# Features in 32-row groups, contexts of the second attention in four column tiles, late expert loads by ScalarE, and new orders in a two-layer language-model tower

## The reference, cut to what matters

```python
h = take(table, x)                                    # 16 sequences of 128 tokens, 256 channels
h = h + attn0(layernorm(h))                           # causal linear attention, 16 heads of 16: elu+1 features
h = h + ffn0(layernorm(h))                            # one 256x256 product, scaled weights
h = h + attn1(layernorm(h))                           # below
h = h + moe(layernorm(h))                             # shared expert and top-1 of 8 experts

def softmax_kernel(x, proj, is_query):                # attn1's features: 16 heads x 64
    xp = einsum('bhnd,md->bhnm', x * 16 ** -0.25, proj)
    diag = sum(square(x), -1, keepdims=True) * 0.5 * 0.25
    stab = max(xp, -1) if is_query else max(xp, (-1, -2))
    return (exp(xp - diag - stab) + 1e-4) / 8
k_sum = sum(kp, axis=2)
denom = einsum('bhnm,bhm->bhn', qp, k_sum)
ctx = einsum('bhnm,bhnd->bhmd', kp, v)
out = einsum('bhnm,bhmd->bhnd', qp, ctx) / denom
x = layer_norm(video + out @ Wo.T + bo, g2, be2)      # then relu MLP of width 1024 and layer_norm again

score = sigmoid(max(logits)); xs = x * score          # moe
h = silu(xs @ gate_e) * (xs @ up_e); moe_out = h @ down_e     # e = argmax of the logits
return moe_out + (silu(x @ shared_gate) * (x @ shared_up)) @ shared_down
```

## Time and profile before

| | |
|---|---|
| runs of the kernel before | 719.12, 720.42, 721.68 us, median 720.42 |
| the profiled execution's own time | 719.09 us |
| its span, first to last instruction | 717.3 us |
| mean granted TensorE clock | 0.979 of full |
| TensorE, VectorE, ScalarE, GpSimd busy | 666.2, 488.2, 282.2, 272.2 us |
| tower; experts | to about 566 us; 151 us |

### The profile page before, as it was taken

The page is one execution under the profiler, slowest core; times in us unless marked ns, Lnnn a source line. Parts: engine busy times, 40 slices in busy tenths (PEclk is TensorE's granted clock), DMA queues, the critical chain, the costliest instruction groups (busy, mean ns, idle before and its releaser), DMA issues.

```text
span 717.3 us, 15031 instructions
## 1 busy us (share of the span) xinstructions
PE 666.2 (93%) x5626; PEld 545.7 (76%) x5627; DVE 488.2 (68%) x1116; ACT 282.2 (39%) x664; POOL 272.2 (38%) x422
## 2 busy tenths in 40 slices
PE   3879899999999999999999999999938699999996
PEld 3667688888898898989888898899937365565654
DVE  1888999999889888888878977867525122323231
ACT  2345456546454462636355263454201032322221
POOL 6244344525426153342504325314201344454542
PEclk9999999999999999999999999999979799999998
DMA  7940000000011010000000000000063411012110
GB/s 266 417 181 9 2 10 8 9 9 9 8 17 16 17 9 16 1 16 9 9 16 1 17 8 9 17 16 8 9 191 117 119 38 48 27 41 66 54 54 11
DMA packets 17296, 34.18 MB, mean 48 GB/s; under 512 B 7617, under 2 KB 12240, under 8 KB 15952
## 3 DMA queue, kind: packets, MB, share of 16 engines
q1 hardware_dynamic: 12640, 24.89, 10.0%
q0 software_dynamic: 4592, 8.41, 4.7%
HBM read 28.74 MB, written 7.29 MB: 50 GB/s over the span
## 4 chain that ended last, share of the span: by engine, by line
PE 79%; DVE 7%; DMA 4%; issue 4%; POOL 3%; ACT 2%; SPq 0%; POOLq 0%; DVEq 0%; ACTq 0%
PE ps L1070 74%; PE ps L1075 2%; DMA x_rows<-send_x 2%; PE ps L1240 2%; DMA sorted_ids<-tokens,slot_u 1%; DVE S_sb L770 1%; DVE stats L711 1%; ACT qkA L687 1%; POOL rstd L412 1%; ACT yTB L677 1%; POOL H L380 1%; POOL preC L471 0%; DMA yA<-x_rows,ids 0%; POOL sorted_ids L483 0%; DVE yA L716 0%
## 5 line engine op out<-in xcount | busy, mean ns | idle before, releaser
L411 POOL TENSOR_TENSOR var_eps<-mv,ln_eps 128x1 f32<-128x1 f32 x112 | 27.7, 248 | 270.3 <-DVE mv L712 269.6
L1070 PE MATMUL ps<-yTC,we 128*128 128x128 f32 x1024 | 125.3, 277 | 0.5 <-DVE yTA L798 0.5
L1070 PEld LDWEIGHTS ps<-yTC,we 128*128 128x128 f32 x1024 | 120.5, 194 | 1.4 <-issue 1.0
L1070 PE MATMUL ps<-we,yTA 128*128 128x256 f32 (+1 forms) x288 | 96.9, 469 | 3.1 <-issue 1.5
L1070 PEld LDWEIGHTS ps<-we,yTA 128*128 128x128 f32 x288 | 54.3, 199 | 27.7 <-issue 22.1
L1070 PE MATMUL ps<-we,yTB 128*128 128x256 f32 (+1 forms) x216 | 71.8, 466 | 0.0
L412 POOL TENSOR_TENSOR rstd<-var_eps,pow_half 128x1 f32<-128x1 f32 x112 | 64.4, 575 | 8.8
L1070 PE MATMUL ps<-we,ffT 128*128 128x256 f32 x256 | 62.0, 385 | 0.0
L1070 PEld LDWEIGHTS ps<-we,yTB 128*128 128x128 f32 x216 | 40.3, 190 | 23.8 <-issue 21.0
L1070 PEld LDWEIGHTS ps<-we,ffT 128*128 128x128 f32 x256 | 46.2, 190 | 8.2 <-issue 3.2
L770 DVE TENSOR_TENSOR S_sb<-ps,causal_sb 128x512 f32<-128x512 f32 x64 | 40.5, 678 | 8.1 <-PE ps L1070 8.1
(11 more groups left out here) (183 smaller groups left out, 1329.1 us busy)
## 6 DMA issues: line engine op xcount, KB each, us to landing
...
x_rows<-send_x SPq DMA_DIRECT2D x16, 128.0 KB, 1.7
home_rows<-send_home SPq DMA_DIRECT2D x16, 128.0 KB, 1.7
...
we<-w_experts SPq DMA_DIRECT2D x3, 512.0 KB, 3.9
we<-w_qk SPq DMA_DIRECT2D x2, 512.0 KB, 3.7
...
```

The source lines that it names most:

```text
L411: link(pool.tensor_tensor(var_eps[:, k:k + 1], mv[:, k, 1:2], ln_eps[:], ALU.add))
L1070: return pe.matmul(o, a, b, start=start, stop=stop)
```

## The change

- `features` works in four groups of 32 rows with proj_sb as a block diagonal of two heads (32 rows, 128 columns). b_k and b_q become one step b_kq with 16 matmuls; the features fill half of each of banks 0 to 3 for K and the other half for Q (xka, xkb). b_rk copies them in two instructions, b_qs reduces and subtracts in two halves each.
- The contexts have [v, 1] of a head (32 columns) as stationary value and its 64 K features as moving one, in four column tiles: one step b_ctx with 16 matmuls. The result is transposed the wrong way round, so ScalarE copies it (b_cT), and two transposes (b_cTT) bring it to ctxp, from where b_cx and b_cx2 copy as before.
- a_den does both halves in one matmul of 256 columns: 8 matmuls.
- free_b, free_ff, free_ga, free_up and free_dn move from SyncE's list to ScalarE's, the loads with them.
- Constants other than four are set by VectorE. TensorE runs 48 f16 matmuls into a free bank before its first step.
- All lists get new orders and lags (TensorE's largest lag is 11, so 27 passes), PSUM a new map, and the `after` waits are laid anew to suit.

```diff
+    WARMING = 48
...
-        proj_sb = sb("proj_sb", [P, 4 * M])
+        proj_sb = sb("proj_sb", [P, 2 * M])
...
-        voB = sb("voB", [P, PAIRS, 2, 32])
+        voB = sb("voB", [P, HEADS, 2, DH])
...
+        ctxT_sb = sb("ctxT_sb", [P, D])
...
-        dgT, T0, qk0, v0, nd0, o0 = (ps[:, 7, :], ps[:, 0, :], ps[:, 3, :], ps[:, 5, :], ps[:, 4, :], ps[:, 3, :])
-        T2, ff0, T3, qk1, v1, dg = (ps[:, 3, :], ps[:, 7, :], ps[:, 6, :], ps[:, 6, :], ps[:, 7, :], ps[:, 6, :])
-        ctxp, nd1, o1, T5, fa, fb = (ps[:, 0, :], ps[:, 0, :], ps[:, 2, :], ps[:, 7, :], ps[:, 7, :], ps[:, 2, :])
-        f2, T6, lo, ga, up, cn = (ps[:, 3, :], ps[:, 7, :], ps[:, 5, :], ps[:, 4, :], ps[:, 2, :], ps[:, 5, :])
-        dn, km, kb = (ps[:, 1, :], ps[:, 5, :], ps[:, 6, :])
-        sc = [ps[:, 6, :], ps[:, 5, :], ps[:, 1, :], ps[:, 2, :]]
-        xk = ps[:, 6:8, :]
-        xq = ps[:, 0:2, :]
+        dgT, T0, qk0, v0, nd0, o0 = (ps[:, 7, :], ps[:, 6, :], ps[:, 6, :], ps[:, 7, :], ps[:, 3, :], ps[:, 4, :])
+        T2, ff0, T3, qk1, v1, dg = (ps[:, 6, :], ps[:, 2, :], ps[:, 4, :], ps[:, 4, :], ps[:, 5, :], ps[:, 6, :])
+        ctxp, ctxT, nd1, o1, T5, fa = (ps[:, 7, :], ps[:, 5, :], ps[:, 4, :], ps[:, 4, :], ps[:, 1, :], ps[:, 7, :])
+        fb, f2, T6, lo, ga, up = (ps[:, 5, :], ps[:, 6, :], ps[:, 5, :], ps[:, 2, :], ps[:, 0, :], ps[:, 1, :])
+        cn, dn, km, kb = (ps[:, 3, :], ps[:, 3, :], ps[:, 7, :], ps[:, 7, :])
+        sc = [ps[:, 5, :], ps[:, 0, :], ps[:, 1, :], ps[:, 2, :]]
         qT = ps[:, 1:3, :]
+        xka = ps[:, 0:2, :]
+        xkb = ps[:, 2:4, :]
...
-                (5, home_out), (0, free_ff), (4, free_ga), (8, ids3), (7, ids1), (2, x_out), (3, ids0), (3, free_up),
-                (2, free_b), (5, free_dn), (7, ids2),
+                (0, x_out), (8, ids2), (2, ids0), (5, ids1), (3, home_out), (8, ids3),
...
-                (7, r4), (4, pA), (6, hC), (10, scat), (4, r1), (4, r2), (1, gat), (0, r0), (8, r5), (4, pA2),
-                (8, r6), (4, r3), (5, pB), (7, pC),
+                (6, pA2), (5, pA), (8, r4), (7, pB), (11, scat), (7, hC), (6, r3), (9, r5), (5, r1), (8, pC), (9, r6),
+                (1, r0), (5, r2), (1, gat),
...
+            def b_cT(t):
+
+                act.wait_ge(S["ctxT_psum"], t + 1)
+                act.activation(ctxT_sb[:], ctxT[:, 0:D], ACT.Copy).then_inc(S["ctxT_ready"], 1)
...
-                act.wait_ge(S["xk_psum"], t + 1)
-                after(act, "ctx_psum", t)
-                act.activation(flat(kf[:]), flat(xk), ACT.Copy).then_inc(S["xk_read"], 1)
+                act.wait_ge(S["xkq_psum"], t + 1)
+                for half, banks in enumerate((xka, xkb)):
+                    act.activation(by_bank(kf, half), banks[:, :, D:2 * D], ACT.Copy).then_inc(S["xk_read"], 1)
...
+            def load_experts(first, last, done):
+                for e in range(first, last):
+                    act.dma_start(we[:, e * EXPERT:(e + 1) * EXPERT], w_experts[e]).then_inc(S[done], 16)
+
+            def free_b(t):
+
+                if t == T - 1:
+                    act.wait_ge(S["ffn0_psum"], T)
+                    act.wait_ge(S["out1_psum"], T)
+                    load_experts(RESIDENT, freed_by_b, "experts_loaded")
+
+            def free_ff(t):
+
+                if t == T - 1:
+                    act.wait_ge(S["ff2_psum"], 2 * T)
+                    load_experts(freed_by_b, freed_by_ff, "experts_loaded")
...
-                (6, b_cx2), (1, a_x), (9, c_tt), (5, b_dgc), (4, a_yT2), (10, c_th), (7, c_ra), (9, c_send),
-                (7, c_rb), (0, a_yT), (5, b_ek), (4, b_yT), (5, b_keps), (1, a_exp), (2, a_rd), (8, c_yT2), (5, b_eq),
-                (6, c_yT), (4, b_x), (4, b_sq), (5, b_rqT), (1, a_par), (4, b_rk),
+                (10, c_th), (2, a_rd), (5, b_cT), (4, b_yT), (8, c_tt), (1, a_par), (0, a_yT), (5, b_rqT), (4, b_x),
+                (5, b_cx2), (4, b_sq), (0, a_x), (4, b_dgc), (4, b_rk), (6, c_ra), (3, a_yT2), (13, free_dn),
+                (8, c_send), (6, c_rb), (5, free_b), (4, b_ek), (4, b_keps), (12, free_up), (7, free_ff), (0, a_exp),
+                (7, c_yT2), (11, free_ga), (4, b_eq), (5, c_yT),
...
-                x = xq.rearrange("p b (h m) -> p (b h) m", m=M)
-                dve.wait_ge(S["xq_psum"], t + 1)
-                link(dve.tensor_reduce(qmax[:, 0, :], x, AX.X, ALU.max))
+                dve.wait_ge(S["xk_read"], t * 2 + 2)
+                halves = [banks[:, :, 0:D].rearrange("p b (h m) -> p b h m", m=M) for banks in (xka, xkb)]
+
+                def heads_of(v, half):
+                    return v[:, 8 * half:8 * half + 8].rearrange("p (b h) -> p b h", b=2)
+                dve.tensor_reduce(heads_of(qmax[:, 0, :], 0), halves[0], AX.X, ALU.max).then_inc(S["dve_step"], 1)
+                counted()
+                link(dve.tensor_reduce(heads_of(qmax[:, 0, :], 1), halves[1], AX.X, ALU.max))
                 dve.wait_ge(S["diag_read"], t + 1)
                 link(dve.tensor_tensor(by_group(qmax[:, 1, :]), by_group(qmax[:, 0, :]), diag_of(0), ALU.add))
-                dve.tensor_tensor(qf[:], x, by_head(qmax[:, 1, :], M), ALU.subtract).then_inc(S["qexp_in"], 1)
+                for half in range(2):
+                    dve.tensor_tensor(by_bank4(qf, half), halves[half],
+                                      heads_of(qmax[:, 1, :], half).unsqueeze(3).broadcast_to([P, 2, 4, M]), ALU.subtract
+                                      ).then_inc(S["qexp_in"], 1)
...
-                (4, a_o), (7, b_o), (6, b_vo), (6, b_ks), (5, b_norm), (10, table1), (6, b_qs), (7, b_x1),
-                (0, a_stats), (2, a_max), (4, a_res), (11, c_hid), (2, a_elu), (2, a_vz), (10, table2), (8, c_o),
-                (3, a_rec), (4, a_norm2), (0, a_norm), (3, a_mean), (6, b_cx), (9, c_log), (9, c_choose), (5, b_km),
-                (8, c_res), (2, a_m1), (10, table3), (2, a_m3), (2, a_m0), (6, b_rec), (5, kmx), (2, a_m2),
-                (6, b_mean), (8, c_norm), (5, b_dgr), (9, c_slot), (4, a_ff), (10, c_gc), (9, table0), (11, c_down),
+                (10, c_norm), (7, b_ks), (7, b_vo), (8, b_x1), (11, c_slot), (12, table2), (13, c_hid), (6, a_ff),
+                (9, c_o), (5, a_o), (6, b_norm), (3, a_elu), (11, table0), (12, table3), (10, c_log), (9, c_res),
+                (12, c_gc), (1, a_stats), (3, a_vz), (5, a_res), (4, a_rec), (5, a_norm2), (4, a_mean), (3, a_m1),
+                (11, table1), (7, b_cx), (3, a_m2), (3, a_m3), (13, c_down), (3, a_m0), (1, a_norm), (10, c_choose),
+                (7, b_rec), (2, a_max), (7, b_mean), (6, b_dgr), (6, b_km), (6, b_qs), (6, kmx), (7, b_o),
...
-                for half in range(2):
-                    for a in range(2):
-                        for b in range(4):
-                            ins = matmul(nd0[32 * b:32 * b + 32, D + half * P:D + half * P + P], flat(den_oneA[:, a]),
-                                         S_sb[:, b, 2 * half + a, :], a == 0, a == 1)
+                for a in range(2):
+                    for b in range(4):
+                        ins = matmul(nd0[32 * b:32 * b + 32, D:2 * D].rearrange("p (h n) -> p h n", h=2), flat(den_oneA[:, a]),
+                                     S_sb[:, b].rearrange("p (h a) n -> p a h n", a=2)[:, a], a == 0, a == 1)
...
-            def features(banks, first_chunk):
+            def features(at, first_chunk):
 
                 for c in range(KD):
-                    for g in range(2):
-                        rows_of = slice(64 * g, 64 * g + 64)
-                        ins = matmul(banks[:, g, c * 4 * M:(c + 1) * 4 * M],
+                    for g in range(4):
+                        rows_of = slice(32 * g, 32 * g + 32)
+                        ins = matmul((xka, xkb)[g // 2][:, g % 2, at + c * P:at + c * P + P],
                                      qkB[rows_of, first_chunk + c, :], proj_sb[rows_of, :], True, True)
...
-            def b_k(t):
+            def b_kq(t):
 
                 if t == 0:
                     pe.wait_ge(S["weights_scaled"], 3)
                 pe.wait_ge(S["qk1_ready"], t * 4 + 4)
-                features(xk, KD).then_inc(S["xk_psum"], 1)
-
-            def b_q(t):
-                pe.wait_ge(S["qk1_ready"], t * 4 + 4)
-                if t + 5 < T:
-                    after(pe, "src0T_ready", t + 6)
-                after(pe, "tile_done", t - 5)
-                features(xq, 0).then_inc(S["xq_psum"], 1)
+                if t + 3 < T:
+                    after(pe, "scores_masked", (t + 3) * 4 + 3)
+                after(pe, "tile_done", t - 6)
+                features(D, KD)
+                features(0, 0).then_inc(S["xkq_psum"], 1)
...
-            def contexts(t, quarter):
-
-                for pair in range(2 * quarter, 2 * quarter + 2):
-                    ins = matmul(ctxp[:, pair * 64:pair * 64 + 64], flat(kf[:])[:, pair * P:(pair + 1) * P],
-                                 flat(voB[:, pair_of(pair)]), True, True)
-                return ins
-
-            def b_ctx0(t):
```

(37 more changed lines are left out.)

161 lines of the change are left out of this document (65 added, 96 removed).

## The result

The changed kernel takes 699.59 us, the median of 4 runs (697.74 to 699.69), against 720.79 for the kernel before on the same chip: ratio 0.970, 95% interval 0.968 to 0.973. Forecast were 678 us, 662 to 700. So the change is faster, as said, but by 21 us and not by 42; the profiled execution took 697.74 us, 20.7 more than the 677 of the sum.

A forecast was written before the change was run, and what follows sets the result against it. TensorE's list was taken to bound the full passes, with VectorE close behind. Passes 20, start 2, tail 19 and experts 1 us sum to 42 off 719.1, giving 677, stated as a median of 678; range 662 to 700.

The forecast's parts named there:

- the sum on TensorE: Per tile, features, contexts, denominators and switches together take 2.0 us off TensorE's list, ends 1.3 and 2.5.
- Features: K and Q features on TensorE: two stints, 2.1 us together, become one of 1.0 us, -1.1 a tile.
- Contexts: Contexts on TensorE: 1.7 us becomes 0.7, two new transposes cost 0.23, net -0.8 a tile.
- Rival C: Loads of 32-row groups in the features don't overlap: +1.0 us a tile for -1.1, 701 us; chance 0.02.
- Full passes of about 30.5: Sign of being right: full passes of TensorE shrink from 31.9 us to about 30.5.
- the friction of 4: Given back for VectorE and TensorE coupling: some 0.5 us in eight or nine passes, 4 us in all.
- rival A: VectorE or the coupling of in-order engines sets the passes: their 20 us go, 698 us; chance 0.15.
- Start: Kernel start: memsets moved to VectorE 1.1 us, early matmuls 1.8; 2 us taken of 2.9, ends 0 and 3.
- Tail: Between tower and experts: x_rows store loses the 12 us above its median, about 4 us idle left; gain 19.
- x_rows over 8 us: Sign of being wrong: the x_rows store at the end of the tower again takes over 8 us.
- rival B: Loads still hold the small stores through shared DMA engines: 12 us of the tail stay, 690 us; chance 0.10.
- What is late next: In the tail, the scatter, ids and gather chain or expert 7's last third holds the end, about 4 us idle.

The follow-up runs named there:

- no_warming: The changed kernel without the 48 f16 matmuls at the start: 700.36 us, ratio 0.9741 to the kernel before.
- ff_first: The changed kernel with free_ff at the head of ScalarE's list, ahead of c_send(14): 695.74 us, ratio 0.9682 to the kernel before.
- before_loads_act: The kernel before with only its late expert loads moved from SyncE to ScalarE: 711.02 us, ratio 0.9868.
- no_ff_load: The changed kernel without the 3 MB of loads of experts 5 and 6 that free_ff issues: 682.37 us, ratio 0.9492 to the kernel before.
- no_late_scatter: The changed kernel without the id scatters of tiles 13 and 14: 690.11 us, ratio 0.9600 to the kernel before.
- loads_on_sp: The changed kernel with the five late-load steps back in SyncE's list, ahead of the stores: 692.66 us, ratio 0.9634 to the kernel before.
- spread_loads: The changed kernel with late loads in SyncE's list, cut to what is free and issued earlier: 683.00 us, ratio 0.9500 to the kernel before.

## Why the prediction was right and where it was wrong

- **What bounds the kernel, and the sum on TensorE: right.** -2.0 us a tile was forecast and 2.0 measured: TensorE is busy for 29.94 us of a full pass, 31.90 before. Features -1.1 forecast, 1.0 measured (two stints of 1.06, now one of 1.11). Contexts 1.7 to 0.7 and 0.23 forecast; 0.45 and 0.27 measured, better by 0.2, and below the 0.5 that the prediction took for their floor. Denominators 1.0, 0.98 measured. Rival C (701 us) had the loads of 32-row groups stand one behind the other; they took 186 ns each and 1.0 us for all 32, so they overlap. The Trainium skill, page "TensorE: Matmul & The Clock Gate", section "LDWEIGHTS (loading the stationary operand)", has a load of 32x128 take as long as one of 128x128. The trace agrees (186 ns, and 190 to 193 with 128 rows); what this does not settle is how many loads run side by side, and that decided here.
- **Full passes of about 30.5: right**, four of 30.1 and one of 31.6; the eight passes gave 12.4 us where the sum had 16 less most of the friction of 4. The early passes gave 3.5 for 2.7. In the full passes VectorE was not the bound (rival A), but it has a microsecond of room left and no more.
- **Start: too small**, 4.5 for 2, though fewer rows lie before the cut. The one row that was used, 3.72 for 1.9 us, was only the first stint; in no_warming the first scores are slow too (2.09 us for 1.15), but so they are in ff_first, with the matmuls. no_warming puts 1 to 4 us on the matmuls, where 1.8 was forecast.
- **Tail: wrong, and most of the miss.** To the last f2 the kernel gained 23.6 us for 22 forecast, and behind it lost 2.2 where 20 were to be gained. With the 6.6 us that only moved across this cut, the tail and the experts account for some 16 of the 20.7 us, and the kernel ahead of the last f2 for some 5. The step that failed reads "with the loads on ScalarE's queue, x_rows no longer stands behind 3 MB of its own queue: the 12 us above its median go". The row of 13.7 us was put down to a queue; before_loads_act puts 8.3 us of the tail down to SyncE's wait at free_ff, ahead of the store, and no_ff_load, no_late_scatter and loads_on_sp put the length of the store itself down to the 3 MB and the scatters on the DMA engines, whichever queue they stand in. The text had named x_rows over 8 us as the sign of being wrong. That is **rival B**, priced at 690 with a chance of 0.10; its mechanism was the true one, its price too low. It had 12 us stay, but the stores grew from 13.7 to 19.2 us. The row that spoke against it, a scatter of 10.0 us beside a load of 1.5 MB, was one of few small pieces beside one load, not 128 pieces beside 256. What the prediction took there from the Trainium skill, page "DMA: Bandwidth & Descriptors", section "Issuing engines are not separate DMA queues", held here: stores on SyncE's queue beside loads on ScalarE's took 18.3 and 19.2 us.
- The tail in terms: 24 us were forecast, 48.3 measured. Idle time 19.3 for 4: 15.3. TensorE's list in the tail 26.2 us (its busy time in spread_loads, where the granted clock there is 0.98) for 19.6, a figure that the prediction gave without its working: 6.6, since the new order leaves more work behind the last f2, which the prediction took over unchanged. Half clock after the hole, 29.05 less 26.19: 2.9. The first and the last of these say that a hole costs more than its length: after it 16 matmul instructions took 3.75 us where 1.95 is usual.
- **What is late next: right, but it only came when the loads were dealt with otherwise.** scatter 6.8, ids 2.7 and gather 2.3 hold the end in spread_loads.
- **The number.** 699.6 lies 0.4 us inside the edge of the range, an edge that was set by rivals A and B. That the range held is owed to its width: one of the signs of being wrong, x_rows over 8 us, came true.
- **Experts: 2.2 for 1.** Their clock rose from 0.96 to 0.99 over the stretch.

Open: why pieces are slow for some 10 us after a scatter of 4-byte pieces. That they are fast when the scatters are left out is shown; the reason is not. Also open is how loads_on_sp gains 3 to 4 us on ff_first at about the same start of the loads.
